# Layer norm of the next token slab placed inside the K projection of the current one, squares moved to VectorE

## What is computed

```python
def _layernorm(x, axis=-1, eps=1e-5):
    m = jnp.mean(x, axis=axis, keepdims=True)
    v = jnp.var(x, axis=axis, keepdims=True)
    return (x - m) / jnp.sqrt(v + eps)

xn = _layernorm(x)
k = proj(Wk, bk)          # xn @ Wk.T + bk, 16 heads of 128
v = proj(Wv, bv)
q = proj(Wq, bq)
s = attention(q, k, v) @ Wo.T + bo
g = silu(ffn(xn))         # fwht, W_up, W_gate, silu, fwht, W_down
return x + s * g
```

## Time and profile before

| | us |
|---|---|
| time before, median of 2 runs | 5262.57 (5257.93 to 5267.2) |
| the profiled execution, as a run | 5257.93 |
| its span, first to last instruction, core 0 (slowest) | 5256.4 |
| spans of the eight cores | 5226.5 to 5256.4 |
| PE busy in the span | 3501.0 (67%) |
| DVE busy | 1818.2 (35%) |
| ACT busy | 1095.2 (21%) |

### The profile page before, as it was taken

The page is one execution under the profiler, slowest core; times in us unless marked ns, Lnnn a source line. Parts: engine busy times, 40 slices in busy tenths (PEclk is TensorE's granted clock), DMA queues, the critical chain, the costliest instruction groups (busy, mean ns, idle before and its releaser), DMA issues.

```text
span 5256.4 us, 62351 instructions; the slowest of 8 cores (5226.5 to 5256.4 us)
## 1 busy us (share of the span) xinstructions
PE 3501.0 (67%) x22715; PEld 1859.8 (35%) x22715; DVE 1818.2 (35%) x3536; ACT 1095.2 (21%) x2987; POOL 293.5 (6%) x309
## 2 busy tenths in 40 slices
PE   0565656566565652777888868299999990081887
PEld 0344445444454531322222227144444430030333
DVE  0222222222222234066667750600000008998001
ACT  0111112111111121134444432111111150000000
POOL 0000000000000000000000000011111110010111
PEclk9977878778787765877777779599999995595999
DMA  9211112111121115221211123188888850091999
GB/s 129 30 28 29 33 25 34 28 29 33 25 35 27 29 29 80 48 54 33 48 33 33 33 35 91 20 77 76 77 77 76 77 56 0 0 136 29 178 180 165
DMA packets 633744, 296.37 MB, mean 56 GB/s; under 512 B 520675, under 2 KB 610787, under 8 KB 631267
## 3 DMA queue, kind: packets, MB, share of 16 engines
q0 software_dynamic: 422880, 191.55, 32.1%
q10 hardware_dynamic: 102912, 58.74, 4.0%
q1 hardware_dynamic: 107652, 42.10, 3.6%
HBM read 433.54 MB, written 50.33 MB: 92 GB/s over the span
## 4 chain that ended last, share of the span: by engine, by line
PE 60%; DVE 22%; issue 4%; DMA 4%; ACT 4%; SPq 3%; another core or an unknown queue 2%; DVEq 1%; ACTq 0%; POOLq 0%
PE pb L835 17%; PE pb L462 10%; PE pb L499 8%; PE pb L674 5%; PE pb L657 5%; PE pb L971 4%; DVE xn_scr L444 4%; PE pb L653 3%; DVE C L919 3%; DVE xnT L448 3%; DMA wdring<-wdT 3%; DVE C L921 3%; SPq L306 3%; PE pb L739 2%; PE pb L548 2%
## 5 line engine op out<-in xcount | busy, mean ns | idle before, releaser
L835 PE MATMUL pb<-xnTf,wring 128*128 128x512 bf16 x4096 | 885.7, 380 | 0.8 <-ACT xnTf L805 0.8
L462 PE MATMUL pb<-xnT,wk_b 128*128 128x128 bf16 x8192 | 512.4, 230 | 436.3 <-DVE xnT L448 436.3
L971 PE MATMUL pb<-U,wdring 128*128 128x512 bf16 x2048 | 465.0, 390 | 423.4 <-DVE U L931 247.3
L462 PEld LDWEIGHTS pb<-xnT,wk_b 128*128 128x128 bf16 x8192 | 506.9, 104 | 445.6 <-issue 444.8
L686 DVE SCALAR_TENSOR_TENSOR pb<-mwin_s,slopes_l,pb 128x256 f32<-128x256 f16 x1019 | 483.5, 482 | 450.6 <-PE pb L674 431.2
L835 PEld LDWEIGHTS pb<-xnTf,wring 128*128 128x128 bf16 x4096 | 401.0, 98 | 485.5 <-issue 3.2
L696 ACT ACTIVATE ET<-pb 128x256 bf16<-128x256 f32 x1019 | 389.8, 383 | 485.5 <-DVE pb L686 391.1
L499 PE MATMUL pb<-wv_b,xnT 128*128 128x512 bf16 x2048 | 447.3, 379 | 0.0
L971 PEld LDWEIGHTS pb<-U,wdring 128*128 128x128 bf16 x2048 | 202.5, 100 | 685.7 <-issue 462.4
L512 DVE TENSOR_TENSOR vstg<-pb,bvB 128x512 bf16<-128x512 f32 x128 | 88.5, 692 | 901.8 <-PE pb L499 901.8
L859 DVE TENSOR_TENSOR U<-A_st,B_st 128x1024 bf16<-128x1024 f32 x64 | 78.4, 1225 | 822.1 <-ACT B_st L851 822.1
(11 more groups left out here) (85 smaller groups left out, 2581.0 us busy)
## 6 DMA issues: line engine op xcount, KB each, us to landing
wdring<-wdT POOLq DMA_DIRECT2D x128, 512.0 KB, 9.1
wring<-wupT POOLq DMA_DIRECT2D x64, 512.0 KB, 8.1
wring<-wgT POOLq DMA_DIRECT2D x64, 512.0 KB, 8.1
xTb<-xT POOLq DMA_DIRECT2D x32, 512.0 KB, 8.4
k_scr<-kstg ACTq DMA_DIRECT2D x32, 512.0 KB, 4.0
v_scr<-vstg ACTq DMA_DIRECT2D x128, 128.0 KB, 1.8
kh<-k_scr SPq DMA_DIRECT2D x16, 1024.0 KB, 5.0
vh<-v_scr SPq DMA_DIRECT2D x16, 1024.0 KB, 9.5
```

What stands on the lines that cost most here:

```text
L462: ins = eng.matmul(bank[:, 0:128], wk_b[:, (ft * H + hch) * 128:(ft * H + hch) * 128 + 128], xnT2[par][:, ft * 128:ft * 128 + 128], start= ...
L835: ins = eng.matmul(pb[bk0 + u][:, 0:UCH], wring[slot][:, ft * 128:ft * 128 + 128], xnTf[:, ft * TOKF + u * UCH:ft * TOKF + u * UCH + UCH], ...
L971: ins = eng.matmul(pb[bk0 + e4][:, 0:FHT], wdring[slot][:, iti * 512 + e4 * 128: iti * 512 + e4 * 128 + 128], Uap(it, tk0, FHT), start=(it ...
```

## The change

The body of the slab loop is split into three functions.

- `ln_head(slab)`: load, squares, stats matmuls, rows, variance, square root, reciprocal. The squares are now one DVE instruction over 128x2048 bf16 instead of 16 on ACT.
- `ln_tail(slab)`: the broadcast matmuls, ACT's two copies, DVE's normalisation.
- `emit_kv(slab, tail_for)`: K and V of a slab, the same operations and waits as before, with `ln_tail(tail_for)` called right after the OP of K chunk 1.

A new loop calls them so that K and V run one slab behind: head(0), tail(0); then for i = 1 to 32: head(i), K and V of slab i - 1 with tail(i) between K chunks 1 and 2; then for i = 33 to 39 head(i), tail(i).

```diff
-    for slab in range(NSLAB):
+    def ln_head(slab):
...
-        def p1_sq(eng, par=par):
-            for ft in range(FT):
-                ins = eng.activation(sq_scr[:, ft * 128:ft * 128 + 128],
-                                     xTb[par][:, ft * 128:ft * 128 + 128],
-                                     AF.Square)
-            return ins
-        ev_sq = OP("scalar", p1_sq,
-                   waits=[ev_ld[slab], ev_sqmm.get(slab - 1)])
...
+        ev_sq[slab] = OP("vector", (lambda eng, par=par: eng.tensor_mul(
+            sq_scr[:], xTb[par][:], xTb[par][:])),
+            waits=[ev_ld[slab], ev_sqmm.get(slab - 1)])
...
+        ev_rstd[slab] = OP("vector", p1_rstd, waits=[ev_sd])
+
+    def ln_tail(slab):
...
         ev_bc = OP("tensor", p1_bc,
-                   waits=[ev_rstd, ev_bcast_ev.get(slab - 1), ev_ones])
+                   waits=[ev_rstd[slab], ev_bcast_ev.get(slab - 1), ev_ones])
...
+        if slab >= NSLAB_A:
+            ev_cons_all[slab] = ev_sqmm[slab]
+
+    def emit_kv(slab, tail_for):
...
+            ev_kc[hch] = OP("tensor", p1_k,
+                            waits=[ev_xnt[slab], ev_wv, wprev])
+            if hch == 1 and tail_for is not None:
+                ln_tail(tail_for)
...
+    for i in range(NSLAB):
+        ln_head(i)
+        if i == 0:
+            ln_tail(0)
+            continue
+        kvslab = i - 1
+        if kvslab < NSLAB_A:
+            emit_kv(kvslab, tail_for=i)
         else:
-            ev_cons_all[slab] = ev_sqmm[slab]
+            ln_tail(i)
+    if NSLAB_A == NSLAB:
+        emit_kv(NSLAB - 1, tail_for=None)
```

More of the change, by code:

```diff
@@ L361, in build_program @@
     ev_ld = {}
+    ev_sq = {}
     ev_sqmm = {}
     ev_rows = {}
+    ev_rstd = {}
     ev_bcast_ev = {}
@@ L380, in build_program, with p1_stats @@
             eng.dma_start(xTb[p].rearrange("p (t c) -> p t c", t=FT),
-                          s[:, c:c + 128].rearrange("(t p) c -> p t c", p=128))),
+                          s[:, c:c + 128].rearrange("(t p) c -> p t c",
+                                                    p=128))),
             waits=[ev_xnt.get(slab - 2),
                    ev_bvB if slab <= 1 else None], dma=psem)
-        def p1_sq(eng, par=par):
-            for ft in range(FT):
-                ins = eng.activation(sq_scr[:, ft * 128:ft * 128 + 128],
-                                     xTb[par][:, ft * 128:ft * 128 + 128],
-                                     AF.Square)
-            return ins
-        ev_sq = OP("scalar", p1_sq,
-                   waits=[ev_ld[slab], ev_sqmm.get(slab - 1)])
-        def p1_stats(eng, par=par, ev_sq=ev_sq):
+        ev_sq[slab] = OP("vector", (lambda eng, par=par: eng.tensor_mul(
+            sq_scr[:], xTb[par][:], xTb[par][:])),
+            waits=[ev_ld[slab], ev_sqmm.get(slab - 1)])
+        def p1_stats(eng, par=par, ev_s=ev_sq[slab]):
             for ft in range(FT):
@@ L398, in p1_stats @@
                            start=(ft == 0), stop=(ft == FT - 1))
-            eng.wait_ge(sch.sems[ev_sq[0]], ev_sq[1])
+            eng.wait_ge(sch.sems[ev_s[0]], ev_s[1])
             for ft in range(FT):
@@ L426, in p1_rstd @@
             return eng.tensor_mul(mrstd_row[:], m_row[:], rstd_row[:])
-        ev_rstd = OP("vector", p1_rstd, waits=[ev_sd])
+        ev_rstd[slab] = OP("vector", p1_rstd, waits=[ev_sd])
+    def ln_tail(slab):
+        is_ffn = slab >= NSLAB_A
+        cc0 = (slab - NSLAB_A) * 128 if is_ffn else slab * 128
+        par = slab % 2
         def p1_bc(eng):
@@ L454, in build_program @@
                                  ev_cons_all.get(slab - 2)])
[L456 to L527, removed]
-        else:
-            ev_cons_all[slab] = ev_sqmm[slab]
@@ new lines, in ln_tail, with p1_k, p1_kev, p1_kdma @@
+        if slab >= NSLAB_A:
+            ev_cons_all[slab] = ev_sqmm[slab]
+    def emit_kv(slab, tail_for):
+        par = slab % 2
+        ev_kc = {}
+        for hch in range(H):
+            def p1_k(eng, hch=hch, par=par):
+                bank = pb[2 + (hch % 2)]
+                for ft in range(FT):
+                    ins = eng.matmul(
+                        bank[:, 0:128],
+                        wk_b[:, (ft * H + hch) * 128:(ft * H + hch) * 128 + 128],
+                        xnT2[par][:, ft * 128:ft * 128 + 128],
+                        start=(ft == 0), stop=(ft == FT - 1))
+                return ins
+            wprev = (ev_kevac.get((slab, hch - 2)) if hch >= 2
+                     else ev_kevac.get((slab - 1, H - 2 + (hch % 2))))
+            ev_kc[hch] = OP("tensor", p1_k,
+                            waits=[ev_xnt[slab], ev_wv, wprev])
+            if hch == 1 and tail_for is not None:
+                ln_tail(tail_for)
+            def p1_kev(eng, hch=hch, par=par):
+                bank = pb[2 + (hch % 2)]
+                return eng.activation(
+                    kstg[par][:, hch * 128:hch * 128 + 128],
+                    bank[:, 0:128], AF.Identity,
+                    bias=bk_l[:, hch:hch + 1])
+            ev_kevac[(slab, hch)] = OP(
+                "scalar", p1_kev,
+                waits=[ev_kc[hch],
+                       ev_kdma.get(slab - 2) if hch == 0 else None])
+        def p1_kdma(eng, slab=slab, par=par):
+            dst = k_dram[:, :, slab * 128:slab * 128 + 128].rearrange(
+                "h d t -> d h t")
+            return eng.dma_start(dst,
+                                 kstg[par].rearrange("p (h t) -> p h t",
+                                                     h=H))
+        ev_kdma[slab] = OP("scalar", p1_kdma,
+                           waits=[ev_kevac[(slab, H - 1)]],
+                           dma="kd%d" % par)
+        ev_vc = {}
+        for vch in range(VCH):
+            def p1_v(eng, vch=vch, par=par):
+                bank = pb[4 + (vch % 2)]
+                for ft in range(FT):
+                    ins = eng.matmul(
+                        bank[:, 0:512],
+                        xnT2[par][:, ft * 128:ft * 128 + 128],
+                        wv_b[:, ft * E + vch * 512:ft * E + vch * 512 + 512],
+                        start=(ft == 0), stop=(ft == FT - 1))
+                return ins
+            wprev = (ev_vevac.get((slab, vch - 2)) if vch >= 2
+                     else ev_vevac.get((slab - 1, VCH - 2 + (vch % 2))))
+            ev_vc[vch] = OP("tensor", p1_v,
+                            waits=[ev_xnt[slab], ev_wv, wprev])
+            def p1_vev(eng, vch=vch):
+                bank = pb[4 + (vch % 2)]
+                return eng.tensor_add(vstg[vch % 2][:], bank[:, 0:512],
+                                      bvB[:, vch * 512:vch * 512 + 512])
+            ev_vevac[(slab, vch)] = OP(
+                "vector", p1_vev,
+                waits=[ev_vc[vch], ev_bvB,
+                       ev_vdma.get((slab, vch - 2)),
+                       ev_vdma.get((slab - 1, VCH - 2 + (vch % 2)))])
+            def p1_vdma(eng, slab=slab, vch=vch):
+                dst = v_dram[slab * 128:slab * 128 + 128,
+                             vch * 512:vch * 512 + 512]
+                return eng.dma_start(dst, vstg[vch % 2][:])
+            ev_vdma[(slab, vch)] = OP("scalar", p1_vdma,
+                                      waits=[ev_vevac[(slab, vch)]],
+                                      dma="vd%d" % (vch % 2))
+        ev_cons_all[slab] = ev_vc[VCH - 1]
```

## The result

| | before | changed |
|---|---|---|
| executions compared, us | 5257.9 to 5301.4 (8 of 12) | 4635.2 to 4689.4 (5 of 14) |
| most of these lie within | 5257.9 to 5267.2 (7) | 4635.2 to 4642.2 (3) |
| ratio of the executions compared, 95% interval | | 0.8837 [0.8796, 0.8879] |
| span of core 0 in the profile | 5256.4 | 4626.5 |

A forecast was written before the change was run, and what follows sets the result against it. It took a serial layer-norm chain, not an engine, as phase 1's bound. Periods of 35.1 us instead of 54.71 gave -600.5 us, the last slabs +14.4: span 5256.4 to 4670, forecast 4673 us, range 4620 to 4735.

The forecast's parts named there:

- The serial chain: Phase 1, each slab: one engine works at a time; 24.99 us of the 54.71 us period are layer norm with nothing behind it.
- The squares: Head of each slab: one DVE product taking 2.29 us, replacing 3.30 us on ACT; square matmuls start at 3.46 us, not 4.88.
- lower end: Price of the DVE squares from the slope of its fastest tensor-scalar rows: 0.56 ns per element, 1.31 us.
- Rival A: Squares priced at the lower end: 0.98 us gained in each of 31 periods and 6 last slabs, about 4635 us; chance 0.30.
- Row chain: Rows, root and reciprocal, from the square matmuls' end to the broadcast: unchanged at 3.26 us.
- The stall of 0.3 us at K chunk 3: K chunk 3 waits for the bank of K chunk 1, whose evacuation stands behind ACT's two copies: 0.3 us.
- rival B: Clock falls in the new gaps, 1.5 to 3.0 us per period: 4719 to 4766 us, in half the periods 4696 to 4720; chance 0.20.
- The start: Start of phase 1: head(1) now precedes K(0), so V(0) ends at about 220.8 us instead of 216.35, +4.5.
- The last slabs: Slabs 33 to 39, without K and V as cover: squares queue behind normalisation, 22.4 us each, 138.9 against 124.5, loss 14.4 us.
- C: Clock stays at 1.2 GHz through K and V because gaps recur: 818 us more, about 5490 us; chance 0.01.
- D: All eight cores dense at once held at 13/16 clock: 6.3 us more per period, near 4870 us; chance 0.02.
- E: The overlap does not come about, since some wait names more than it should: within 20 us of 5262; chance 0.01.

The follow-up runs named there:

- Experiments 1: The kernel before with only the squares changed, to one DVE instruction, and no reordering: 5184.0 to 5189.8 us, ratio 0.9842 to the kernel before.
- experiment 2: The changed kernel with the 16 squares back on ACT, the new order kept: 4720.5 and 4721.1 us, ratio 0.8957 to the kernel before.
- experiment 3: The changed kernel with the squares reading and writing the same elements at step 2: 4719.8 us, 4777.4 in the profiled execution, ratio 0.9010 to the kernel before.
- Experiment 4: The changed kernel with 22 and 26 unneeded matmuls in front of the waits for squares and broadcast: 4634.1 to 4647.0 us, ratio 0.8806 to the kernel before.
- experiment 5: The changed kernel with the next slab's broadcast and normalisation behind K chunk 3 instead of chunk 1: 4589.0 and 4592.4 us.
- Experiment 7: The changed kernel with the squares of slabs 33 to 39 back on ACT: 4608.4 to 4622.2 us, ratio 0.8725 to the kernel before.
- experiment 6: The changed kernel with load, squares and stats matmuls one slab earlier, between V chunks: 4535.2 us twice, 4567.7 profiled, ratio 0.8595 to the kernel before.
- experiment 8: The changed kernel with the head one slab earlier and squares of slabs 34 to 39 on ACT: 4502.4 to 4517.5 us, ratio 0.8526 to the kernel before.

## Why the prediction was right, and where its terms were off

**What bounds it: right.** The serial chain was the bound. The change took 20.4 us from the mean period (54.62 to 34.21), and what phase 1 lost came out at the end of the span. Experiments 1 and 2 divide it: the order gives 17.0 us of a period with the squares on either engine, the squares 3.3 to 3.4 with either order; as ratios, the order alone 0.8957, the squares alone 0.9842.

**The squares: the term that was mis-sized.** I took the tensor-tensor line of the earlier trace rows, 2.29 us, where it measured 1.21, below even my lower end of 1.31. Rival A is what happened, and experiment 3 shows that it hangs on the step: step 2 gives 2.41. That is what the Trainium skill says in "VectorE: DVE Perf Modes" (two elements per cycle for a tensor-tensor of dense 16-bit tensors, 1224 ns for 2048). The trace agrees, with 1215 ns. The rows that I took instead all have an f32 operand. That the lower end came near was luck in part, since it was a slope through two rows of 16 and 64 elements of another operation. DVE also began the squares at 0.86 us of the period and not 1.03, just before the row of the V evacuation ended (764.91 + 0.69). Together the square matmuls start at 2.21 instead of 3.46: 1.25 us in 31 periods, 39 us.

**Row chain, broadcast, K, V: right.** Row chain 771.19 - 767.92 = 3.27 us (3.26); wait before the broadcast 1.37 (1.64); broadcast to K chunk 2 0.61 (0.60); V 13.90 (13.91). The stall of 0.3 us at K chunk 3 does not show as a wait: K chunks 2 to 15 took 12.62 us against my 12.8.

**The clock: rival B in part.** I forecast full clock and allowed 1.5 to 3 us per period if it fell. It fell in 8 to 10 of 31 periods, at a cost of 1.53 us each, on core 0 together 10 x 1.53 = 15 us. Experiment 4 shows that the gaps cause it, and experiment 5 that the first of them alone does not. This partly cancelled the cheap squares: a short period is 1.42 us under my sum of 35.08, 44 us in 31, and with the clock's 15 and 2 of smaller delays the mean period came out at 34.21, 27 us in all.

**The start: 4.5 us too late.** V(0) ended at 216.32 us, not 220.8: the cheap squares count twice here, and the first mean matmuls, which wait for the first load, started at 160.98 instead of 162.98. Nothing in the change explains these 2 us; in the same execution this start lies between 156.1 and 162.4 us on the eight cores.

**The last slabs: right in sign, 9 us too high.** I predicted 138.9 us from V(31)'s end, a loss of 14.4; it was 129.5, a loss of 5.0. The difference is again the squares: 1.08 us for each slab, and their earlier start. Experiment 7 shows the step itself, that the squares queue behind DVE's normalisation.

Sum: 4670 - 27 - 4.5 - 9.4 = 4629, against a span of 4626.5. From 4670 to the forecast I made a slip: with the 1.5 and 4.6 us that I named it is 4676, not 4673. And that the measured time falls on the 4635 of rival A is luck in part: the squares and the last slabs were cheaper than A had them, and the falls of the clock, which A had not, gave 15 us back.

**Rivals C, D, E.** C and E did not come. For D: in experiment 6 PE is busy for 930 us without a pause, on core 0 at 1.00, and in experiment 8 all eight cores read 1.00 over the same 930 us with PE busy for 919 to 930 of them. So all cores dense at once do not by themselves bring the level that D took from the Trainium skill ("TensorE: Matmul & The Clock Gate", Part 1, the caveat on the peak-current limiter). But a level of 0.81, which is 13/16, does appear in these traces: on core 6 in the profile of the changed kernel, then on core 4 in experiment 6, where the second row has the same work at 1.00.

```profile
2950.00:3300.00 350.00, 350.00 (x1335) 144.99 (x1334) 25.73 (x21) 51.85 (x82) 46.80 (x41) 0.81 0.67 64
```

```profile
220.00:400.00 180.00, 178.58 (x1757) 129.96 (x1766) 73.35 (x201) 34.21 (x104) 5.71 (x5) 0.81 0.28 45
450.00:1150.00 700.00, 693.71 (x7928) 510.96 (x7972) 337.16 (x918) 154.85 (x469) 26.26 (x23) 1.00 0.33 53
```

So the level is there, but dense cores are not enough for it here, and it does not last as long as the load. I gave D 0.02 on the ground that the dense stages of the one profile that I had were at 1.00. What sets it off was not tried.

## What to carry to other kernels

When an engine's idle time is a chain of short steps on other engines, let its next independent work stand in its queue in front of the step that ends the chain (here this took 17 us off each period, and the head one slab earlier still another 3.2). Moving work to another engine has to be checked in every stretch: the squares gained 3.4 us in a period where DVE was idle, and cost 23.4 us over the last slabs, where they queued behind the normalisation. And price an elementwise instruction by a row with the same types and the same step, and not by its operation alone.

## What the runs showed of the hardware that I had not expected

- A VectorE product of 128x2048 bf16 took 1.21 us with step 1 and 2.41 with step 2.
- TensorE's clock can fall after gaps far shorter than the 3.8 us of the kernel before: with pauses of 1.16 and 1.37 us, 2.95 us of matmuls between them, it went to 1.2 GHz in 8 to 10 of 31 periods, with 2.36 us in all of them, and with the pause of 1.16 us and one of 0.19 in none (experiment 5). A low stretch cost 1.53 us when it fell on dense K matmuls, and 1.2 us, though it was longer, when it fell where PE would have waited (experiment 2).
- Unneeded matmuls in the gaps kept the clock up (experiment 4) and cost 0.14 us in a period; they left a gain of 0.36 us in a period that does not show in the time of the slowest core. Removing the gaps (experiment 6) gave 3.24.
- The granted clock of a core with TensorE busy throughout read 1.00 in most stretches and 0.81 in some: in the profile of the changed kernel on cores 4 to 7 alike from 3000 to 3150 us, where cores 0 to 3 read 1.00. It went back to 1.00 under the same load (experiment 6, core 4).
